# Cross attention with 32x32 block transposes on VectorE and score products over 32 rows each, in a kernel of attention, recurrence and experts

## What is computed

```
hc  = layernorm(x)                                  # 64 x 512 a batch
Sim = (hc @ w1)[:, :, None] + (ctx @ w2)[:, None, :] + einsum('bid,bjd->bij', hc * w3, ctx) + b_sim
A   = softmax(Sim, axis=2)
hq_hat = einsum('bij,bjd->bid', A, ctx)
Batt   = softmax(max(Sim, axis=2), axis=1)
hc_bar = einsum('bi,bid->bd', Batt, hc)
feats  = [hc, hq_hat, hc * hq_hat, hc * hc_bar]
x1     = x + feats @ W_qv + b_qv                    # W_qv: 2048 x 512
```

## Time and profile before

| | us |
|---|---|
| median of 3 runs (1582.21 to 1584.47) | 1582.35 |
| span of the profiled execution | 1606.2 |
| PE busy in it | 1417.7 |
| POOL busy in it | 756.1 |
| DVE busy in it | 721.5 |
| ACT busy in it | 377.6 |
| body-to-body distance in the cross attention (15 bodies) | 50.43 |

### The profile page before, as it was taken

The page is one execution under the profiler, slowest core; times in us unless marked ns, Lnnn a source line. Parts: engine busy times, 40 slices in busy tenths (PEclk is TensorE's granted clock), DMA queues, the critical chain, the costliest instruction groups (busy, mean ns, idle before and its releaser), DMA issues. The chain is left out here.

```text
span 1606.2 us, 28597 instructions
## 1 busy us (share of the span) xinstructions
PE 1417.7 (88%) x9329; PEld 914.6 (57%) x9330; DVE 721.5 (45%) x1715; ACT 377.6 (24%) x716; POOL 756.1 (47%) x592
## 2 busy tenths in 40 slices
PE   5899999999999999999998777898549999996960
PEld 3455555555555555555546556666438888885750
DVE  2443434434344344443437776787583233231221
ACT  1322222322223222232215412222301111111110
POOL 0134431444214442144406855787495886806830
PEclk9999999999999999999998999999679999998985
DMA  9514542244422444224406569532103333314322
GB/s 331 191 53 147 177 177 92 107 154 176 172 96 99 162 176 161 107 92 169 170 7 224 165 242 318 176 111 97 66 27 131 137 137 131 139 57 144 117 67 103
DMA packets 94905, 225.10 MB, mean 140 GB/s; under 512 B 9448, under 2 KB 25960, under 8 KB 94864
## 3 DMA queue, kind: packets, MB, share of 16 engines
q1 hardware_dynamic: 85136, 191.02, 34.0%
q0 software_dynamic: 9200, 32.51, 5.8%
q10 hardware_dynamic: 528, 1.05, 0.2%
HBM read 179.20 MB, written 45.35 MB: 140 GB/s over the span
## 5 line engine op out<-in xcount | busy, mean ns | idle before, releaser
L487 DVE COPY ctxT<-T 128x512 f32<-128x512 f32 (+1 forms) x208 | 139.6, 671 | 251.4 <-PE T L353 251.4
L487 ACT COPY ctxT<-T 128x512 f32<-128x512 f32 (+1 forms) x208 | 118.7, 570 | 450.0 <-PE T L353 450.0
L390 PE MATMUL S<-ctxT,qT 128*64 128x384 f32 (+2 forms) x1280 | 211.7, 448 | 0.0
L318 POOL TENSOR_TENSOR xb<-x_sb,bqv_b 128x512 f32<-128x512 f32 x16 | 20.3, 1272 | 256.9 <-DMA x<-xb 256.9
L331 POOL TENSOR_TENSOR wb<-wb,x 128x2048 f32<-128x2048 f32 x30 | 135.5, 4538 | 0.0
L353 PEld LDWEIGHTS T<-ident,ctx_one 128*128 128x128 f32 (+1 forms) x896 | 92.0, 141 | 63.6 <-ACT ctxT L487 34.9
L315 POOL TENSOR_TENSOR rstd<-ve,mhalf 128x1 f32<-128x1 f32 x16 | 8.8, 551 | 252.7 <-DVE nmean L573 252.7
L353 PE MATMUL T<-ident,ctx_one 128*128 128x128 f32 (+1 forms) x896 | 116.9, 273 | 0.0
L327 POOL TENSOR_TENSOR wb<-w,hcb 128x2048 f32<-128x2048 f32 x30 | 107.5, 3606 | 19.1 <-DVE w12L L646 19.1
L1881 POOL TENSOR_TENSOR w_high<-w_low,f_zero 128x2048 fp32r<-128x2048 f32 x21 | 96.8, 4609 | 36.3 <-DMA w_low<-_L_ffn_gate_up_proj_dram 24.7
L1932 PE MATMUL f_Dn<-w_high,f_hH 128*128 x156 | 67.9, 435 | 49.6 <-issue 48.0
(11 more groups left out here) (299 smaller groups left out, 2925.0 us busy)
## 6 DMA issues: line engine op xcount, KB each, us to landing
x<-in_ctx_dram SPq DMA_DIRECT2D x32, 768.0 KB, 7.3
ctx_one<-in_ctx_dram SPq DMA_DIRECT2D x32, 768.0 KB, 5.6
ctx_two<-in_ctx_dram SPq DMA_DIRECT2D x32, 768.0 KB, 7.3
ctx_one<-in_ctx_dram SPq DMA_DIRECT2D x32, 512.0 KB, 5.4
w_low<-_L_ffn_gate_up_proj_dram POOLq DMA_DIRECT2D x10, 1024.0 KB, 8.3
f_xt<-routed_x SPq DMA_DIRECT2D x39, 256.0 KB
routed_y<-f_yt SPq DMA_DIRECT2D x39, 256.0 KB
ctx_one<-in_ctx_dram SPq DMA_DIRECT2D x32, 256.0 KB
```

The lines of the kernel that those rows point to most:

```text
L390: last = pe.matmul(S[64 * b:64 * b + 64, k, col:col + w], qT[:, c, 64 * b:64 * b + 64], buf[:, b, c, 0:w], start=(c == 0), stop=(c == C - 1))
L487: copy(buf[:, bank, :, i * P:i * P + rows], T[bank][:].rearrange("p (c j) -> p c j", c=C)[:, :, 0:rows]).then_inc(t_free[bank], 1)
```

## The change

- **Transposes.** PE's transposes of the context and their copies by ACT and DVE are gone. DVE's block transpose turns every 32x32 block of a tile from SBUF to SBUF, two tiles in one instruction (the tail tile alone): 12 + 2 instructions a pair. After it, partition group a (32 partitions) of `ctxA` or `ctxB` holds 32 features of 32 of a tile's 128 rows, for each of 16 feature blocks.
- **Scores.** `scores` now has three blocks (4, 5 and 4 tiles). For each of 16 feature blocks k, each row group a and each batch b it does one product over 32 rows with 64 stationary and 128 or 160 moving columns: 384 products a pair, eight next to each other on eight parts of the array. Row group a writes PSUM bank a of S. Their count is 40 before. `probs` lies in `ctxB`.
- **Queries.** Each row group needs all 16 feature blocks of q. ACT makes q (in `f3`), writes it to DRAM, waits for that, and reads it back four times with 32 rows each, into `qr`.
- **Order.** The norm of the next pair moves from DVE to the end of ACT's body, its power to POOL after `wb`. The first block of the next pair's transposes moves into the tail of DVE's body. The row maximum is taken in one go after all scores. `hqhH` and `f2H` share `hfH`, `hqhL` and `f2L` share `hfL`: so the second pair is made only after the first 12 of Y's products (`y1_done`).
- **Loads.** `ctx_two` has four tiles, `ctx_one` nine, loaded in four parts, freed after value positions 1, 4, 6 and 8. Of the gates stage's two early loads the weights come second.

The diff, cut to its core:

```diff
-BLOCKS = [(0, 3, 0, 0), (3, 3, 1, 0), (6, 3, 2, 0), (9, 2, 3, 0), (11, 2, 3, 256)]
+BLOCKS = [(0, 4, 0), (4, 5, 8), (9, 4, 4)]
+AV_ORDER = [*range(4, 13), *range(0, 4)]
+PARTS_ONE = [(4, 2, False), (6, 2, True), (8, 2, False), (10, 2, False)]
+PART_ENDS = [1, 4, 6, 8]
...
-            def scores(j, p, f, fs, loads, step):
-                for c in range(C):
-                    if j + 1 < NBLK and c < BLOCKS[j + 1][1]:
-                        turn_ctx(j + 1, 2 * c, p, fs, loads, step)
-                        turn_ctx(j + 1, 2 * c + 1, p, fs, loads, step)
-                    for b in range(2):
-                        last = pe.matmul(S[64 * b:64 * b + 64, k, col:col + w], qT[:, c, 64 * b:64 * b + 64],
-                                         buf[:, b, c, 0:w], start=(c == 0), stop=(c == C - 1))
+            def scores(j, f):
+                buf = (ctxA, ctxB)[j % 2]
+                pe.wait_ge(turned[j], f + 1)
+                if j == 0:
+                    pe.wait_ge(q_in, 64 * (f + 1))
+                    pe.wait_ge(exp_done, EXPS * f)
+                for k in range(DB):
+                    c, e = k // QUADS, k % QUADS
+                    for a in range(QUADS):
...
+                        for b in range(2):
+                            last = pe.matmul(S[64 * b:64 * b + 64, a, col * Q:col * Q + w], qr[a * Q:(a + 1) * Q, e, c, 64 * b:64 * b + 64],
+                                             buf[a * Q:(a + 1) * Q, b, k, 0:w], start=(k == 0), stop=(k == DB - 1))
...
                     for c in range(C):
-                        product(c, hqhH, hqhL, c, c == 0, False)
+                        last = product(c, hfH, hfL, c, c == 0, False)
+                    last.then_inc(y1_done, 1)
                     pe.wait_ge(wb_step, 4 * (p + 1))
...
+            def norm(f):
+                act.wait_ge(nr_ready, f + 1)
+                act.activation(tok_rows[:], x_sb[:], ACT.Identity, scale=rstd[:, 0:1], bias=nr[:, 0:1]).then_inc(hc_ready, 1)
...
+                    for c in range(C):
+                        act.activation(f3[:, c, :], hcT[fs][:, c, :], ACT.Identity, scale=w3T[:, c:c + 1],
+                                       bias=w2T[:, c:c + 1]).then_inc(q_made, 1)
+                    act.dma_start(q_d, f3[:].rearrange("p c i -> p (c i)")).then_inc(q_out, 16)
+                    act.wait_ge(q_out, 16 * (f + 1))
+                    for a in range(QUADS):
+                        act.dma_start(qr[a * Q:(a + 1) * Q].rearrange("p e c i -> p e (c i)"),
+                                      q_d.rearrange("(e r) d -> r e d", r=Q)).then_inc(q_in, 16)
...
+            def turn_two(buf, src, i, b, col):
+                return dve.transpose(buf[:, b, :, col * Q:(col + 2) * Q].rearrange("p k (t r) -> p t k r", r=Q),
+                                     src[:, i:i + 2, :].rearrange("p t (k r) -> p t k r", r=Q))
...
+            def row_max(f):
+                dve.wait_ge(qk_done, NBLK * (f + 1))
...
                 if front:
-                    drain_ctx(dve, copy, 1, 1, p, fs, step)
+                    turn_second(f)
+                if loads is not None:
+                    norm_stats(f + 1)
+                if back:
+                    dve.wait_ge(hqhH_ready, p + 1)
+                    dve.tensor_tensor(hfL[:], T[0][:].rearrange("p (c i) -> p c i", c=C), hfH[:].bitcast(F32),
+                                      ALU.subtract).then_inc(hqhL_ready, 1)
...
+                if front:
+                    turn_third(f, 0)
+                    turn_third(f, 1)
+                if back:
+                    dve.wait_ge(f2H_ready, p + 1)
+                    dve.tensor_tensor(hfL[:], f3[:], hfH[:].bitcast(F32), ALU.subtract).then_inc(f2L_ready, 1)
+                if front:
+                    row_max(f)
...
+                    if loads is not None:
+                        turn_first(f + 1, s if back else 1, loads, 0)
```

More of the change, by code:

```diff
@@ new lines, in values @@
+            def values(p, s, step):
+                pe.wait_ge(hqh_ready, p)
+                for n, pos in enumerate(AV_ORDER):
+                    for q in range(len(AT_TILES)):
+                        if AT_TILES[q][0] == n:
+                            pe.wait_ge(t_free[q % 2], turn(q % 2, f"probs{q}", *before(p)) + 1)
+                    if n == 1:
+                        pe.wait_ge(tcol_ready, p + 1)
+                        fill(1, "trow", p, step)
+                        pe.transpose(T[1][0:1, 0:P], tcol[:], ident[:]).then_inc(t_full[1], 1)
+                    for b in range(2):
+                        rows = tile_rows(pos)
+                        src, i = context(s, b, pos)
+                        last = pe.matmul(O[64 * b:64 * b + 64, :], probsT[0:rows, n, 64 * b:64 * b + 64],
@@ L431, in body @@
                         pe.matmul(Y[:, 0:P], ones1[:], brow[:], start=True, stop=True).then_inc(brow_full, 1)
-                    if back and t in [t0 + n - 1 for t0, n, _, _ in BLOCKS[TWO_SLOTS:]]:
-                        last.then_inc(av_one, 1)
+                last.then_inc(av_done, 1)
+            def body(p, s, step, loads):
+                front, back = step != "last", step != "first"
+                f = p + 1
+                if front:
+                    pe.wait_ge(hc_ready, f + 1)
+                    turn_tile(0, "hc", tok_rows, p, step)
                 if back:
-                    last.then_inc(av_done, 1)
+                    values(p, s, step)
                 if front:
-                    scores(0, p, f, fs, loads, step)
-                    for j in range(1, NBLK - 1):
-                        scores(j, p, f, fs, loads, step)
+                    scores(0, f)
                 if back:
@@ L443, in body @@
                 if front:
-                    scores(NBLK - 1, p, f, fs, loads, step)
+                    scores(1, f)
+                if front:
+                    scores(2, f)
                 if back:
@@ L459, in body @@
                                       start=False, stop=False)
-                    pe.wait_ge(t_free[0], turn(0, "hqh", p, step) + 1)
+                    pe.wait_ge(f2L_ready, p + 1)
                     for c in range(C):
-                        if front and c < 2:
-                            turn_probs(2 + c, p, step)
-                        last = product(c, f2H, f2L, C + c, False, c == C - 1)
+                        if front and c != 2:
+                            turn_probs((1, 2, None, 3)[c], p, step)
+                        last = product(c, hfH, hfL, C + c, False, c == C - 1)
                     last.then_inc(y_done, 1)
@@ L512, in body @@
                 if front:
-                    drain_ctx(act, copy, 0, 0, p, fs, step, only=(0,))
                     act.wait_ge(t_full[0], turn(0, "hc", p, step) + 1)
@@ L560, in _ @@
+            act.wait_ge(const_in, 80)
+            norm(0)
+            bodies(act, body)
         @block.vector
@@ L684, in body @@
-                if front:
-                    dve.wait_ge(exp_done, 4 * f + 4)
-                    dve.tensor_reduce(zsum[:], z4[:], axis=AX.X, op=ALU.add).then_inc(z_done, 1)
+                    if loads is not None:
+                        turn_first(f + 1, s if back else 1, loads, 0)
+                    drain_probs(dve, copy, 0, p, step)
+                    drain_probs(dve, copy, 2, p, step)
+                    if loads is not None:
+                        turn_first(f + 1, s if back else 1, loads, 1)
```

454 lines of the change are left out of this document (216 added, 238 removed).

## The result

The changed kernel takes 1774.15 us (median of 4 runs, 1771.66 to 1782.54) beside 1582.28 for the kernel before in the same comparison: a ratio of 1.1226, interval 1.1196 to 1.1256. The forecast was 1495 with a range to 1580. The range did not hold the time, and the sign was wrong.

A forecast was written before the change was run, and what follows sets the result against it. PE alone was taken to have no slack. Its stream of 36.5 us, plus waits and added costs, gave a 44.5 us body, 5.9 less; 14 steps and 4 at the start save 87 us: 1495 us, range 1445 to 1580.

The forecast's parts named there:

- (a): q's DRAM trips while context parts 1 and 2 land: 4 us a trip, back 1.5 us after the values; 1 added.
- The first rival: PE's loop no longer stays resident, packets at 2.6 us: scores 15.6 us, body 47.8, in all 1545 us; chance 0.16.
- the wait before the last third: PE, two thirds through the scores, waits 2.2 us for DVE's transposes.
- the collision: DVE's `s1` may wait 3.6 us behind POOL's `wb`, 2.1 of it costing PE; a coin, 1 us added.
- The second rival: Score products don't run eight abreast: scores 26.7 us, body 55 to 57.5, about 1665 us; chance 0.18.
- the round of eight: Eight score products side by side on PE take about 0.11 us at 128 columns; all scores 11.3 us.
- double transposes: DVE's block transposes of two context tiles in one instruction: 1.15 us each, bounds 1.0 and 2.3.
- the wait before the first turn of the probabilities: PE, before turning probabilities, waits 2.0 us for the row maximum and first exponential, released by ACT.
- DVE's chain: DVE's work in order during the scores: six transposes and norm done at 17.5 us, four more transposes at 24.2.
- The wait for hc: PE waits 0.8 us for hc, behind the last turn's copy and next norm on ACT at the body's end.
- Longer waits lower the clock: If PE's waits before the last third of scores grow 1.5 us, some 1.5 us more a body: +20 us.
- The start: The first pair's step, with q's two trips under full load: from 8 us gained to 5 lost, 4 gained taken.

The follow-up runs named there:

- e5_hold: Changed kernel, with SP issuing each body's next ctx_one loads only after q is back from DRAM: 1700.63 us, ratio 1.0759 to the kernel before.
- e1_q_pe: Changed kernel, with q spread to the row groups by PE products with identity columns and ACT copies, no DRAM trip: 1646.42 us, ratio 1.0421 to the kernel before.
- e2_k4: Changed kernel with only 4 of the 16 feature blocks in the scores, q still through DRAM: ratio 1.0381 to the kernel before, 54.56 us a body.
- e11_q_k8: `e1_q_pe` with 8 of the 16 feature blocks in the scores: ratio 0.9628 to the kernel before, 47.11 us a body.
- e8_q_k4: `e1_q_pe` with only 4 of the 16 feature blocks in the scores: ratio 0.9660 to the kernel before, 47.69 us a body.
- e7_unrolled: Kernel before the change, with PE's loop written out so that every PE instruction has to be loaded: ratio 0.9996, 50.46 us a body.

## Why the prediction was wrong, by its own steps

- **(a), the q trips: failed.** The row was there, 5.8 us for a store behind loads, and I took 4. The read is issued when the loads of parts 1 and 2 have just filled the queues; it lands after 11.0 us in the median. The write took 5.1 (forecast 4) and ended at 456.99, when 3.8 us of values were left to cover the read; it needed 16.9 until the last of the four reads was in. So PE waited 13.2 us where the prediction had 1.5 and added 1. `e5_hold` (4.5 us with the loads held back) shows the cause, and `e1_q_pe` (no trip) what it cost. A median over loads of all ages was the wrong row for a transfer that always starts just behind new ones.
- **The first rival, instructions: right mechanism, wrong price, and not a rival.** Its condition was met, as the Trainium skill's "Runtime: NRT & Kernel Launch", section "Instruction fetch mechanics", would have it: 2048 instructions don't hold 3500. The trace agrees (76 packets between 200 and 800 us, where before q1 stood alone from 210 on), `e2_k4` agrees from the other side (2 packets), and so does `e11_q_k8`, some 2100 instructions a turn and 62 packets. I gave it 2.6 us a packet; it is 3.5 between two with the transfers idle (and about 6 with them full, in the versions without the q wait). So the scores took 21.0 us and not 15.6. The step that failed is that latency: the time from entering one packet until the next can run, of which the transfer is only 0.96. And the chance of 0.16 was given as if this excluded (a). Both held.
- **The two together.** From the forecast body of 44.5: 12.2 more for q (13.2, of which 1 was in it), 9.7 more for the scores; the wait before the last third (2.2) and the collision (1) lie under the others. That gives 63.2, and 62.38 was measured.
- **The second rival, not eight abreast: wrong mechanism.** It is the only one that had the kernel slower, and that is luck: it had 26.7 us of scores and a body of 55 to 57.5, and 21.0 and 62.38 were measured. 128 records take 2.08 us, and the three stretches of the body shown take 6.4, 6.6 and 7.4 us for the ideal 3.5, 4.3 and 3.5, not by their rounds but by the gaps between packets.
- **Right by the trace:** the round of eight at 0.11 us for 128 columns, read from the earlier trace rows; double transposes at 1.15 us (4.61 for four) for 1.15 forecast; the wait before the first turn of the probabilities, 1.90 for 2.0; `s1` at over 4 us, and its price at zero under a longer wait. From the first third to the last, DVE's chain takes 12.3 us (446.90 to 459.18 in `e11_q_k8`) for the 11.4 forecast. The wait for hc of 0.8 was 0.67 in `e8_q_k4`; after, the loop's jump covers it in the body shown.
- **Longer waits lower the clock: held.** After 13 us the clock stood at 0.50, and 146 records took 4.24 us; at 17 ns each they would take 2.5. These 1.8 us are inside the 21.0.
- **The start:** 15.8 us lost for 4 gained. By the first marks, fewer score records give back 16.0 (64.7 to 48.7, `e2_k4`), the trip alone 8.5 (56.2, `e1_q_pe`), both 23.1 (41.6, `e8_q_k4`), 7.3 less than before the change.
- **What is left of the gain.** With both costs gone the body is 47.1 to 47.7 us, 3 below the kernel before. That is with part of the scores left out, but also with 3.6 us of spreading on PE that the changed kernel doesn't have and with the lower clock behind the waits for DVE (0.50 in `e8_q_k4` from 462 to 465 us). It speaks for the rest of the forecast but doesn't show a body of 44.5.

## What to carry to other kernels

- Count the instructions of a loop before cutting its work into smaller pieces. Here pieces of 32 rows stream well, but 256 instructions were used up in 2 us and came in 3.5, or in about 6 beside context loads; from there on the number of instructions is the price, not their work.
- Price a small transfer on a path that PE waits for by what stands in the queues at the moment when it is issued, not by a median over the run: 4.5 us with them clear, 11.0 behind the context loads. Instruction packets are such transfers too.
- Rivals that don't exclude each other add up. A wait that vanishes in an experiment may only lie under another one: look for its successor before calling it removed.

## What the runs showed that I had not expected

- A stream whose instructions have to be loaded all the time can be nearly free. At 29 packets in 600 us (`e7_unrolled`) no time was lost, at 62 (`e11_q_k8`) hardly any (5.1 us in the longest row of waits); at 92 in 600 (`e1_q_pe`) it was 7.3 us a body.
- No packet moved while PE stood waiting for q from 461 to 474 us: the one before began at 444.5, the next at 476.2, after PE had gone on. The waits of 15.5 and 14.4 us of the next two bodies are as empty. In these three bodies the long wait ahead of dense code was not used to load that code.
- Full transfers hardly lengthen the movement of an instruction packet, they delay its start. In the kernel before, the nine packets of the earlier trace rows move for 1.03 us in the mean (the forecast's 0.96 comes from a share rounded to 0.3%), in the changed kernel all 135 for 1.09, and for 0.92 to 1.02 in the quiet stretch above. But from the start of a piece to the start of the next packet it is 1.1 us beside an idle memory and mostly 2.4 to 5.3 beside a full one; in `e5_hold` 3.2 to 3.5 in 12 of 15 cases. The read of q of 256 KB behind the same loads took 2.4 times as long as without them.
